# A two-layer transformer on one core: expert rows gathered by a list of tokens, and three shared experts behind the routed blocks

## The reference

```python
gu_s = x2 @ shared_w_gate_up.T
g_s, u_s = jnp.split(gu_s, 2, axis=-1)
shared_out = jax.nn.silu(g_s) * u_s @ shared_w_down.T          # inner width 512
probs = jax.nn.softmax(x2 @ gate_w.T, axis=-1)                 # 16 experts
topk_vals, topk_idx = jax.lax.top_k(probs, 2)
...
act = jax.nn.silu(g) * u                                       # inner width 128 an expert
moe_out = jnp.einsum('eth,te->th', out_e, combine)
return (moe_out + shared_out).reshape(orig_shape)
```

## Time and profile before

| | us |
|---|---|
| median of 3 runs | 696.88 |
| the three runs | 700.21, 696.12, 696.88 |
| the profiled execution, whole | 696.53 |
| its span, first to last instruction | 694.8 |

### The profile page before, as it was taken

How to read it: one execution, slowest core, us unless ns; L and a number is a source line. 1 busy time by engine, 2 the same in 40 slices (tenths; PEclk the granted TensorE clock), 3 DMA queues, 4 the chain that set the end, 5 groups by cost and what they waited for, 6 DMA issues and landing times.

```text
span 694.8 us, 13440 instructions
## 1 busy us (share of the span) xinstructions
PE 598.3 (86%) x5108; PEld 473.6 (68%) x5108; DVE 392.2 (56%) x1126; ACT 270.7 (39%) x433; POOL 228.3 (33%) x330
## 2 busy tenths in 40 slices
PE   2998999767889977999999996868799699999984
PEld 1987987656667654776777765646478588888761
DVE  3414644787776766778778785722662243323264
ACT  5165118347754234244353443545410122221213
POOL 6001434354500015454363553551036211110071
PEclk9999999979999987899999997867999899999998
DMA  8941220362234616053361443020029389997365
GB/s 302 381 156 20 47 46 18 84 173 85 49 95 159 189 56 215 32 184 102 114 216 54 163 171 147 4 93 1 1 98 392 116 316 399 417 418 287 148 169 193
DMA packets 49903, 109.62 MB, mean 158 GB/s; under 512 B 12016, under 2 KB 18288, under 8 KB 47664
## 3 DMA queue, kind: packets, MB, share of 16 engines
q1 hardware_dynamic: 30224, 62.73, 25.1%
q0 software_dynamic: 14000, 35.81, 15.8%
q10 hardware_dynamic: 5616, 10.23, 4.2%
HBM read 67.96 MB, written 36.18 MB: 150 GB/s over the span
## 4 chain that ended last, share of the span: by engine, by line
PE 59%; DVE 13%; ACT 10%; issue 7%; DMA 5%; POOL 5%; SPq 1%; POOLq 0%; ACTq 0%; DVEq 0%
PE bank L336 17%; PE bank L517 11%; PE bank L372 9%; ACT FP L1457 4%; DVE FP L922 4%; PE bank L603 4%; PE bank L575 3%; PE bank L588 3%; POOL slots_in L1853 2%; PE bank L719 2%; POOL FP L1865 2%; DVE kraw L1191 2%; PE bank L395 2%; PE bank L383 1%; PE bank L548 1%
## 5 line engine op out<-in xcount | busy, mean ns | idle before, releaser
L1457 ACT ACTIVATE FP<-bank 128x512 f32<-128x512 f32 (+1 forms) x244 | 138.7, 611 | 285.4 <-PE bank L336 103.0
L1191 DVE CUSTOM_DVE_ANT_0 kraw<-bank,maskb 128x256 bf16<-128x256 f32 (+1 forms) x256 | 88.4, 400 | 34.4 <-PE bank L575 34.4
L517 PE MATMUL bank<-W,XR 128*128 128x512 f32 x348 | 99.6, 429 | 1.6 <-DVE XR L922 1.5
L336 PE MATMUL bank<-FP 128*128 128x128 f32 x558 | 88.6, 313 | 0.8 <-ACT FP L1457 0.8
L372 PE MATMUL bank<-W,XR 128*128 128x512 f32 x288 | 77.1, 417 | 5.2 <-DVE W L922 5.2
L517 PEld LDWEIGHTS bank<-W,XR 128*128 128x128 f32 x348 | 66.8, 203 | 16.4 <-DVE XR L922 2.0
L1820 POOL TENSOR_SCALAR_AFFINE_SELECT FP<-FP 128x512 f32<-128x512 f32 x64 | 41.5, 671 | 95.9 <-ACT FP L1457 95.9
L372 PEld LDWEIGHTS bank<-W,XR 128*128 128x128 f32 x288 | 64.0, 271 | 11.6 <-DVE W L922 5.6
L336 PEld LDWEIGHTS bank<-FP 128*128 128x128 f32 x558 | 66.4, 195 | 2.8 <-DVE FP L922 1.6
L922 DVE TENSOR_TENSOR FP<-FP,bank 128x128 f32<-128x128 f32 (+1 forms) x39 | 14.4, 369 | 67.6 <-ACT FP L1457 46.6
L336 PE MATMUL bank<-RP,W 128*128 128x512 f32 x192 | 45.8, 394 | 2.2 <-DVE FP L922 2.2
(11 more groups left out here) (166 smaller groups left out, 995.4 us busy)
## 6 DMA issues: line engine op xcount, KB each, us to landing
FP<-in_experts_dram SPq DMA_DIRECT2D x31, 768.0 KB, 8.3
slots_out<-QS SPq DMA_DIRECT2D x48, 256.0 KB, 2.7
RP<-slots_out POOLq DMA_DIRECT2D x8, 1024.0 KB, 5.4
FP<-slots_in POOLq DMA_DIRECT2D x31, 256.0 KB, 6.7
slots_out<-FP ACTq DMA_DIRECT2D x31, 256.0 KB, 8.1
slots_in<-RP SPq DMA_DIRECT2D x7, 1024.0 KB, 13.2
QS<-slots_out POOLq DMA_DIRECT2D x5, 1024.0 KB, 7.0
XR<-slots_out POOLq DMA_DIRECT2D x3, 1024.0 KB, 5.9
```

What stands on the lines that cost most here:

```text
L336: mm = nc.tensor.matmul(bank, lhs, rhs, start=(n == 0), stop=(n == len(terms) - 1))
L517: mm = nc.tensor.matmul(b[:, :], *terms[n], start=(n == 0), stop=(n == len(terms) - 1))
L1191: ins = nc.vector.tensor_tensor_reduce(masked[:, 2 * (f % 2) + m, 0:n], b[:, m, :], maskb[:, m0:m0 + n], 1.0, -BIG, ALU.add, ALU.max, hmax ...
L1457: return nc.scalar.activation(o, i, func, **kw)
```

## The change

`xs` is now a plain copy of the 1024 rows: SP writes the eight tiles as soon as each is normed. The zeros, the 16 scatters and the waits on them are gone. POOL loads each block with one indirect gather instead of a plain transfer; it reads 128 rows by `index`, which names the token of each slot. `index` is made by a product: DVE (`split_index`, behind shared item 1) builds, for each of the 16 picks of a partition, a row of ones and zeros for the place in the block (`at_place`, 16 x 128) and a pair of rows with the token's tile and lane at its block (`token_of`), PE multiplies them in 16 small matmuls behind `down` of shared item 1, and DVE (`join_index`, behind shared item 2) adds the halves. A slot that no token has gets index 0. Blocks 0 to 30 follow one another, and three shared items of group 1 stand at the end. PE adds tiles 4 and 5 ahead of the last `down` and tiles 6 and 7 behind it.

```diff
--- before.py
+++ after.py
@@ -38,8 +38,8 @@
 TABLE = E + E * E + T + NB
 
 
-ITEMS = ([("shared", 0, e) for e in range(SE)] + [("shared", 1, 0)] + [("block", b) for b in range(NB - 8)]
-         + [("shared", 1, 1)] + [("block", b) for b in range(NB - 8, NB)] + [("shared", 1, e) for e in range(2, SE)])
+ITEMS = ([("shared", 0, e) for e in range(SE)] + [("shared", 1, 0)] + [("block", b) for b in range(NB)]
+         + [("shared", 1, e) for e in range(1, SE)])
 LAST = ITEMS.index(("block", NB - 1))
 
 
...
@@ -713,7 +720,7 @@
 
                 pe.wait_ge(xblock_in[b % XB_], 16 * (b // XB_ + 1))
                 if b == 0:
-                    V.drained(pe, "ranks")
+                    V.drained(pe, "index")
                 bank = XBank.fill(pe, ("xblock", b))
                 for c in range(DC):
                     mm = nc.tensor.transpose(bank[:, c * P:(c + 1) * P], xblock[:, b % XB_, c * P:(c + 1) * P], ident[:, :])
@@ -749,9 +756,12 @@
                     (_, dh), (_, dl) = halves(e)
                     hi, lo = (ah[:, k % 2, a, :] for a in range(2))
                     for j in range(G):
+                        closed = e == SE - 1 and (g == 0 or j < G - 2)
                         for n, (l, r) in enumerate(((hi, dh), (hi, dl), (lo, dh))):
                             mm = nc.tensor.matmul(acc[j][:, :], l[:, j * P:(j + 1) * P], r,
-                                                  start=(e == 0 and n == 0), stop=(g == 0 and e == SE - 1 and n == 2))
+                                                  start=(e == 0 and n == 0), stop=(closed and n == 2))
+                        if g == 1 and closed:
+                            mm.then_inc(routed_added, 1)
                     mm.then_inc(down_done, 1)
                 else:
                     b = ITEMS[k][1]
@@ -774,21 +784,35 @@
                     for t in range(T):
                         nc.tensor.matmul(b[:, (t + 1) * E:(T + 1) * E], onesb[:, :], picked[:, t:t + 1, :].broadcast_to([P, T - t, E]),
                                          start=False, stop=False)
-                    nc.tensor.matmul(b, onesb[:, :], picked[:, T:T + 1, :].broadcast_to([P, T + 1, E]), start=False, stop=True)\
+                    nc.tensor.matmul(b, onesb[:, :], picked[:, T:T + 1, :].broadcast_to([P, T + 1, E]), start=False, stop=True)
+                    nc.tensor.matmul(V.banks[V.number["ranks"] % 2][:, 256:256 + P], onesb[:, :], before[:, :], start=True, stop=True)\
                         .then_inc(V.full, 1)
                 if k >= 1 and k != LAST + 1:
                     down(k - 1)
+                if k == 2:
+                    pe.wait_ge(index_split, 1)
+                    b = V.fill(pe, "index")
+                    for n in range(TOP * T):
+                        mm = nc.tensor.matmul(b[:, 0:2 * NB], at_place[:, n, :], token_of[:, n, :, :],
+                                              start=(n == 0), stop=(n == TOP * T - 1))
+                    mm.then_inc(V.full, 1)
                 if following == ("block", 0):
                     turn(0)
-            down(len(ITEMS) - 1)
-
-            for t in range(G, T):
+
+            def add_routed(t, closed):
                 pe.wait_ge(tile_gathered[t], 16 * TOP)
                 pe.wait_ge(diagonals_ready, TOP * G)
                 for k in range(TOP):
                     mm = nc.tensor.matmul(acc[t - G][:, :], diagonal[:, TOP * (t - G) + k, :], gathered[:, (TOP * t + k) % YG, :],
-                                          start=False, stop=(k == TOP - 1))
-                mm.then_inc(routed_added, 1)
+                                          start=False, stop=(closed and k == TOP - 1))
+                if closed:
+                    mm.then_inc(routed_added, 1)
+
+            add_routed(G, False)
+            add_routed(G + 1, False)
+            down(len(ITEMS) - 1)
+            add_routed(T - 2, True)
+            add_routed(T - 1, True)
 
 
         @block.sync
...
-            def zero_slots(first, last):
-                for b in range(first, last, 4):
-                    n = min(4, NB - b)
-                    sp.dma_start(xs[b * P:(b + n) * P, :].rearrange("(b p) n -> p b n", p=P),
-                                 zeros.rearrange("p (b n) -> p b n", b=4)[:, 0:n, :]).then_inc(zeroed, 16)
-
             load_kernel(0, k0)
-            sp.wait_ge(zeros_ready, 1)
-            zero_slots(0, NB)
 
...
@@ -897,6 +913,9 @@
                 e = nc.sync.value_load(owner[0:1, b:b + 1], min_val=0, max_val=E - 1)
                 sp.dma_start(wblock[b % WB], experts[bass.ds(e, 1), :, :].rearrange("a p n -> (a p) n")).then_inc(wblock_in[b % WB], 16)
 
+            for t in range(T):
+                sp.wait_ge(x_ready, 2 * T + t + 1)
+                sp.dma_start(xs[t * P:(t + 1) * P, :], X[:, t, :]).then_inc(x3_out, 16)
             sp.wait_ge(owner_ready, 1)
             for b in range(WB - 1):
                 load_weights(b)
...
@@ -1346,6 +1363,7 @@
 
 
                 b = V.take(v, "ranks")
+                own(nc.vector.tensor_copy(column, b[:, 256:256 + P]))
                 nc.vector.tensor_copy(ranks, b[:, 0:(T + 1) * E].rearrange("p (t e) -> p t e", e=E)).then_inc(V.free, 1)
                 V.drained(v, "ranks")
                 own(tt(over, spread(ranks[:, T, :], 2, [P, E, T]), spread(full, 1, [P, E, T]), ALU.is_gt))
@@ -1357,6 +1375,7 @@
                     own(tt(oslot[:, k], oh[:, k], ranks[:, 0:T, :], ALU.mult))
                 own(nc.vector.tensor_reduce(slotf, oslot, AX, ALU.add))
                 nc.vector.tensor_copy(slots[:, :, :], slotf).then_inc(slots_ready, 1)
+                own(nc.vector.tensor_scalar(slotp, slotf.rearrange("p k t -> p (k t)"), 1.0 / P, None, ALU.mult))
                 own(tt(ends, base, nblocks, ALU.add))
                 own(tt(passed, spread(ends[0:1, :], 1, [1, NB, E]), spread(block_no[0:1, :], 2, [1, NB, E]), ALU.is_le))
                 own(nc.vector.tensor_reduce(ownf, passed, AX, ALU.add))
@@ -1366,6 +1385,30 @@
                 own(nc.vector.tensor_scalar(tiny[:, 4, :], tiny[:, 3, :], 1.0, None, ALU.add))
                 own(nc.vector.reciprocal(share[:, 0, :], tiny[:, 4, :]))
                 own(tt(share[:, 1, :], tiny[:, 3, :], share[:, 0, :], ALU.mult))
+
+            def split_index():
+
+                shape = [P, TOP * T, NB]
+                own(nc.vector.tensor_reduce(tokenp, before[:, :], AX, ALU.add))
+                own(nc.vector.tensor_scalar(tokenp, tokenp, -1.0, float(P - 1), ALU.mult, ALU.add))
+                own(tt(not_below, spread(slotp, 2, shape), spread(block_no, 1, shape), ALU.is_ge))
+                own(nc.vector.tensor_reduce(blockp, not_below, AX, ALU.add))
+                own(nc.vector.tensor_scalar(blockp, blockp, -1.0, None, ALU.add))
+                own(tt(of_block, spread(blockp, 2, shape), spread(block_no, 1, shape), ALU.is_equal))
+                own(nc.vector.scalar_tensor_tensor(placep, blockp, -1.0, slotp, ALU.mult, ALU.add))
+                own(nc.vector.tensor_scalar(placep, placep, float(P), None, ALU.mult))
+                for k in range(TOP):
+                    n = slice(k * T, (k + 1) * T)
+                    own(tt(token_of[:, n, 0, :], of_block[:, n, :], spread(full, 2, [P, T, NB]), ALU.mult))
+                own(nc.vector.tensor_scalar(token_of[:, :, 1, :], of_block, tokenp, None, ALU.mult))
+                tt(at_place, spread(placep, 2, [P, TOP * T, P]), spread(column, 1, [P, TOP * T, P]), ALU.is_equal).then_inc(index_split, 1)
+
+            def join_index():
+
+                b = V.take(v, "index")
+                nc.vector.tensor_reduce(indexf, b[:, 0:2 * NB].rearrange("p (a b) -> p b a", a=2), AX, ALU.add).then_inc(V.free, 1)
+                V.drained(v, "index")
+                nc.vector.tensor_copy(index[:, :], indexf).then_inc(index_ready, 1)
 
             def collect(tiles, sums):
 
@@ -1408,8 +1451,12 @@
                     tt(ab[:, k % 2, :], sg[:, k % 2, 0:P], bank[:, P:2 * P], ALU.mult).then_inc(A.free, 1)
                 if k == 0:
                     place()
+                elif k == 1:
+                    split_index()
+                elif k == 2:
+                    join_index()
                 if item == ("block", 3):
-                    v.wait_ge(scattered, 16 * TOP * T)
+                    v.wait_ge(x3_out, 16 * T)
                     v.wait_ge(acc_done, G)
                     collect(range(G), [held[:, j, :] for j in range(G)])
                     v.wait_ge(x_summed, G)
...
@@ -1846,16 +1891,14 @@
                     if step == 6 and r < T:
                         stack_maxima(r, 0)
 
-            p.wait_ge(zeroed, 16 * ((NB + 3) // 4))
-            p.wait_ge(slots_ready, 1)
-            for t in range(T):
-                for k in range(TOP):
-                    nc.gpsimd.indirect_dma_start(xs, bass.IndirectOffsetOnAxis(slots[:, k, t:t + 1], 0), X[:, t, :], None).then_inc(scattered, 16)
-            p.wait_ge(scattered, 16 * TOP * T)
```

(6 more changed lines are left out.)

19 lines of the change are left out of this document (11 added, 8 removed).

## The result

The changed kernel took 694.09 us (median of 20 runs, 691.96 to 699.87), the kernel before in the same series 697.89 (20 runs). The ratio is 0.995 with a 95% interval of 0.9929 to 0.9971; a second series gave 695.03 us and 0.9928 (0.9899 to 0.9957). So it is 3.5 to 5 us faster. The forecast was 8.7 us, and 688.2 us: the time lies 0.1 us above the upper end of the range, and the likeliest case, faster by over 1%, did not come.

A forecast was written before the change was run, and what follows sets the result against it. PE was taken as the bound (busy 86% of the span), with the DMA engines also full in the blocks. Front -4.3, moved item -8.5, end +3.6 and slip +0.5 gave -8.7 us, to 688.2 us; range 684.5 to 694.

The forecast's parts named there:

- the likeliest case: Whole kernel: faster by over 1%, that is below 689.9 us; chance 0.63.
- the slip of the ring of `ys`: Blocks: ACT's copy of a block's product, held by the writes of `ys`, slips; +0.5 us (0 to 2).
- the growth of the end: Behind the blocks: with three shared items PE is done at 691.2 instead of 687.6, so +3.6 us.
- the front: Ahead of the blocks' steady stretch: block 2 turned at about 550.2 against 554.52, a gain of 4.3 us.
- the moved item: Between blocks 22 and 25: one shared item moves to the end, so 8.5 us leave the blocks.
- The half-clock window: Front, around block 0's turn: granted clock 0.80, partly 1.2 GHz; the turn priced at 0.6 us at full clock.
- The plain price: Blocks: a gather costs the DMA engines the same as a plain load, 2.5 engine-us a MB.
- the hot row: Nearly empty blocks: unused slots all read one row, slow serving stalls each such block; 704 or 712 us; chance 7%.
- the case that costs 16 us: Blocks: the hot row's load lasts 5.2 us; 10 blocks x 2.1 us - 5 = 16, or 704 us.
- DVE late at the end: End: DVE's 3.51 us idle ahead of tile 4's sum comes again, adding some 2 us: 690; chance 12%.
- dear gathers: Blocks: gathers at 3.6 engine-us a MB make the blocks DMA-bound, +4 us, 692; chance 20%.
- a late front: Front: `split_index` takes 10 us or POOL's chain passes 540, block 0 turned at 546 again: 692; chance 6%.

The follow-up runs named there:

- order_only: The kernel before, its scatter and zeros kept, with only the new order of items and the new adds at the end; ratio 0.995.
- after_spread: The changed kernel with slots of index 0 given a row of their own, so empty slots of a block read different rows; ratio 0.9901.
- pause: y4_late_spread with POOL waiting, after 8 of the 16 last indirect loads, for ACT's last silu; 685.67 us, ratio 0.9823.
- y4_late_spread: The changed kernel with four buffers for the blocks' products, the list made one shared item later, and empty slots reading own rows; 690.78 us, ratio 0.989.
- y4_late_spread_old_order: y4_late_spread with the order of items and the adds at the end as in the kernel before; 692.36 us, ratio 0.9905.

## Why the forecast was wrong, point by point

Two terms of the sum failed: the slip of the ring of `ys` in the blocks, and above all the growth of the end. The other two, the front and the moved item, came as forecast.

**The front: right.** Taken back by 4.46 us, block 0 is turned at 543.17 (543.5 forecast) and block 2 at 549.84 (550.2). `split_index` took 6.9 us as summed, shared item 3 started at 526.74 (527), the list was ready at 528.1 (529). The gain is 4.5 us (4.3). Against the second profile of the kernel before it is 6.3: the old front took 54.0 to 55.9 us in its executions, the new one 49.6 in every one. The half-clock window is gone, as was priced with the turn at 0.6 us.

**The moved item: right.** Without other losses the blocks took 93.7 to 94.3 us, 8 to 8.5 less than before. order_only has it at 94.3.

**Gathers in the blocks: price right, rival mis-sized.** The plain price held. But I gave the hot row a price only as a delay of its own load (what a load lasts beyond 3.084 us, less the 5 us that are covered), and looked only for the case that costs 16 us. I had also counted ten nearly empty blocks; by the same inputs blocks 4, 11 and 23 hold 4, 1 and 1 tokens, so there are thirteen. The first step that failed is the term "0.5 us (0 to 2)" for the slip of the ring of `ys`: the hot row goes into that term, and it measured 2.4 to 3.9 us against after_spread, in which TensorE sees no slip at all. I had both pieces on the page, a ring with no slack and a source of slower transfers beside it, and did not add them.

**The end: the larger step that failed.** The term was +3.6 and measured +7.5. I named "DVE late at the end" as a rival with the right row, DVE idle 3.51 us by "remote", and priced it as the same pause come again, +2. The pause grows: it lasts as long as POOL's series still runs behind TensorE's work, and with one more shared item behind the blocks more of that work falls into the series. It was 7.0 to 8.0 us in seven of eight executions of the new order with the unbroken series, 3.9 in the eighth. It moved the statistics by 6 us, where DVE had 1 to spare, and the end by 3.9: 0.8 us until the last matmul (35.4 against 34.6) and 3.1 behind it (10.3 against 7.2). That is the whole miss of this term. With the break in the series the end is 41.9 and the growth +3.7, as forecast, so the count of TensorE's work was right.

The same 3.9 us can be seen from the other side. My new end (41.8) was worked out as TensorE's work without waits, the old one (38.2) was measured and held them. That is right only if the waits go away in the new order, and they did not: like against like it is 40.5 against 32.8 without POOL's loads, or 45.7 against 38.2 with them, +7.7 and +7.5.

**The sum.** -4.5 - 8.5 + 2.4 to 3.9 + 7.5 = -3.1 to -1.6 by stretches; the medians say -3.5 to -5. The profiles of single executions account for the size of the miss, not for the last 2 us of the gain; the 1.8 us by which the old front differed between two profiles may be part of them, which is not shown. That the time lies only 0.1 us outside the range is no merit of the sum: the range was made for dear gathers and a late front, and neither came.

**Made better.** The run pause keeps the whole result and takes 685.67 us, 1.8% under the kernel before, where the change alone has 0.5 to 0.7%. Its terms are spread rows for the blocks (the fourth buffer adds nothing there that can be seen, 93.7 us with and without it), the list one item later for the front (48.1 instead of 49.6), and the pause for the end. It lies below the 688.2 of the forecast.

## What to carry to other kernels

When work is moved into a stretch, price the stretch before and after by the same rule: a sum of engine work against a measured time with stalls in it takes for granted that the stalls go away. An idle time that the trace puts down to nothing it names is not a constant; find what runs beside it and ask whether it will last longer. Here the padding of a gather list was better pointed at different rows, and the long series of indirect loads wanted a break where other engines hand work to each other.

## What the runs showed of the hardware

**TensorE's semaphores come late during a long series of indirect loads.** In the new order consumers started on time up to the eighth load in a row. The next one, ACT's silu, was due beside the tenth or eleventh load and came 1 to 8.7 us behind TensorE's rows (at 668.83 for a product at about 660.1, in y4_late_spread). DVE then stood idle for 3.9 to 8.0 us, in seven of eight executions until 0.7 to 3 us behind the end of the series. With the loads issued by SP, or with a break of 4 us behind the eighth, it was gone, and the time of unprofiled runs fell by 2 to 7 us, so it is no trick of the records. It does not come every time: in y4_late_spread_old_order, with the same 16 loads in a row, TensorE's adds of tile 5 end at 674.44 and DVE takes them at 674.48, beside the last load of the series.

```profile
672.46 1.98 PE L806 MATMUL bank<-FP 128*128 128x512 f32 x4 [0.33 <-DMA FP<-slots_out,slots]
...
673.67 0.95 POOL L1903 DMA_INDIRECT FP<-slots_out,slots  x1 [0.30 <-issue]
...
674.48 0.69 DVE L934 TENSOR_TENSOR X<-X,bank 128x512 f32<-128x512 f32 x1 [1.05 <-issue]
```

The Trainium skill (Perfetto Trace Analysis, Summary: the profiler window per engine type) says that a matmul's end in the profile is an estimate and that the way of its semaphore is hidden. The wait of a consumer is then the sign to look for, as here. The Trainium skill also says (DMA: Bandwidth & Descriptors, SWDGE vs HWDGE vs iDMA) that GpSimd writes its descriptors into rings in SBUF and that transfers issued by SP and ACT bypass them. That fits the run with SP, but no run here shows what such writes have to do with TensorE's semaphores; the mechanism stays open, and so does why one execution with four buffers waited only 3.9 us and another was on time.

**One row for all.** 31 gathers of 128 times the same 2 KB row lowered the full DMA rate from 418 to 387 GB/s. Gathers of nearly distinct rows ran as fast as plain loads (418 GB/s in both).

**POOL's price of a gather.** 0.96 us to issue a gather against 0.54 for a plain load of the same 256 KB, with 0.30 between two in a row. The 16 at the end take 1.02 us each and so 21 us with the gaps, and in the old order, with its two shared items behind the blocks, TensorE's last adds waited 2.03 us for them.
